# Two-layer graph network on one core: x1's third tile loaded among the attention weights, first residuals behind the weights, third tile's eviction moved

## The reference

```
h  = relu(layernorm(x))
n  = ln_weight * h * rsqrt(mean(h*h) + 1e-6)
g  = n @ W_root + bias + sum over r of (segment_sum of n[src] @ W_rel[r], by dst) / max(count_r, 1)
x1 = x + h + elu(g) @ wo

h  = relu(layernorm(x1))
p  = h @ W
e  = exp(-leaky_relu((p @ a_l)[src] + (p @ a_r)[dst], 0.1))
out = x1 + elu(segment_sum(e * p[dst], by src) / (segment_sum(e, by src) + 1e-5))
```

## Time and profile before

| | us |
|---|---|
| Median of 3 runs | 565.16 |
| The three runs | 562.09, 565.47, 565.16 |
| Profiled execution, whole time | 562.03 |
| Its span | 560.2 |
| PE busy | 529.5 (95%) |
| DVE busy | 401.2 (72%) |
| ACT busy | 226.4 (40%) |
| POOL busy | 74.4 (13%) |
| Granted TensorE clock, mean | 0.992 of full |

### The profile page before, as it was taken

How to read it: one execution, slowest core, us unless ns; L and a number is a source line. 1 busy time by engine, 2 the same in 40 slices (tenths; PEclk the granted TensorE clock), 3 DMA queues, 4 the chain that set the end, 5 groups by cost and what they waited for, 6 DMA issues and landing times.

```text
span 560.2 us, 8076 instructions
## 1 busy us (share of the span) xinstructions
PE 529.5 (95%) x3093; PEld 455.5 (81%) x3094; DVE 401.2 (72%) x662; ACT 226.4 (40%) x418; POOL 74.4 (13%) x69
## 2 busy tenths in 40 slices
PE   3989999999799999999997999999999999999996
PEld 2879898988688889989876888888877888888886
DVE  5846859549899898987486455556489887777643
ACT  5755335215745544445872233222233232222302
POOL 4063112000000000000000000000007222222310
PEclk9999999999899999999998999999999999999999
DMA  9842331303022124122594111110003322222221
GB/s 269 249 148 74 110 111 38 110 15 90 1 71 71 46 74 123 63 75 74 169 331 131 37 38 37 38 37 2 0 1 91 93 74 74 73 74 73 74 75 41
DMA packets 19805, 47.25 MB, mean 84 GB/s; under 512 B 3908, under 2 KB 8387, under 8 KB 19636
## 3 DMA queue, kind: packets, MB, share of 16 engines
q1 hardware_dynamic: 19761, 46.67, 27.5%
HBM read 31.30 MB, written 15.36 MB: 83 GB/s over the span
## 4 chain that ended last, share of the span: by engine, by line
PE 77%; DVE 12%; ACT 6%; DMA 2%; issue 2%; SPq 0%; DVEq 0%; ACTq 0%
PE ps L1178 10%; PE ps L1430 9%; PE ps L1432 8%; PE ps L1431 8%; PE ps L1339 8%; PE ps L1296 6%; PE ps L1412 5%; PE ps L1413 5%; PE ps L1411 5%; PE ps L1394 2%; PE ps L1382 2%; DVE bn L724 2%; PE ps L1384 2%; PE ps L1383 1%; DMA x1t<-x_scratch 1%
## 5 line engine op out<-in xcount | busy, mean ns | idle before, releaser
L1430 PE MATMUL ps<-h_hi,att_hi 125*125 125x512 f32 (+1 forms) x190 | 73.5, 387 | 0.0
L1431 PE MATMUL ps<-h_lo,att_hi 125*125 125x512 f32 (+1 forms) x190 | 72.6, 382 | 0.0
L1432 PE MATMUL ps<-h_hi,att_lo 125*125 125x512 f32 (+1 forms) x190 | 72.5, 382 | 0.0
L1411 PE MATMUL ps<-wg,gT_hi 128*125 128x512 f32 x160 | 64.3, 402 | 0.0
L1412 PE MATMUL ps<-wg,gT_hi 128*125 128x512 f32 x160 | 63.5, 397 | 0.0
L1413 PE MATMUL ps<-wg,gT_lo 128*125 128x512 f32 x160 | 63.4, 396 | 0.0
L1339 PE MATMUL ps<-msg_hi,adj_hi 125*125 125x288 f32 x200 | 55.8, 303 | 0.0
L543 ACT CAST adj_hi<-ps 125x400 fp32r<-125x400 f32 (+1 forms) x65 | 32.1, 494 | 52.4 <-PE ps L1296 51.3
L1339 PE MATMUL ps<-msg_lo,adj_hi 125*125 125x286 f32 x200 | 50.8, 294 | 0.0
L1178 PE MATMUL ps<-w_hi,hT_hi 128*125 128x430 f32 x128 | 46.3, 362 | 0.1
L1178 PE MATMUL ps<-w_hi,hT_lo 128*125 128x430 f32 x128 | 45.8, 358 | 0.0
(11 more groups left out here) (216 smaller groups left out, 1145.5 us busy)
## 6 DMA issues: line engine op xcount, KB each, us to landing
xt<-in_x SPq DMA_DIRECT2D x10, 448.0 KB
xh_scratch<-xt SPq DMA_DIRECT2D x10, 448.0 KB
xt<-xh_scratch SPq DMA_DIRECT2D x10, 448.0 KB
x_scratch<-xt SPq DMA_DIRECT2D x10, 448.0 KB
x1t<-x_scratch SPq DMA_DIRECT2D x10, 448.0 KB
xr<-x_scratch SPq DMA_DIRECT2D x10, 448.0 KB
out_x<-xr SPq DMA_DIRECT2D x19, 224.0 KB
wg_raw<-in_L_gnn_W SPq DMA_DIRECT2D x8, 512.0 KB, 6.2
```

The lines of the kernel that those rows point to most:

```text
L1411: M.matmul(to, hi, wg[k][:, 0, cut], start=n == 0, stop=False)
L1430: M.matmul(to, hi[:, s, :], h_hi[:, s, cut], start=s == 0, stop=False)
L1431: M.matmul(to, hi[:, s, :], h_lo[:, s, cut], start=False, stop=False)
L1432: return M.matmul(to, lo[:, s, :], h_hi[:, s, cut], start=False, stop=s == TILES - 1)
```

## The change

1. SP loads x1's tile 2 behind the first two attention weights, and tile 3 ahead of the store of x1's tile 9, instead of behind all of them.
2. POOL waits before its first residual until seven of the eight parts of `w_lo` are done.
3. In stage 1, tile 2's eviction (`transposed(2, 0, 1)`) and tile 0's messages stand ahead of the mean squares of tiles 2 and 3 on ACT; DVE's reciprocal of tile 2's mean square stands behind tile 0's messages.
4. At the seam, DVE does the statistics of tile 2 (`variance2`, then `deviation2`) and tile 1's `gT_lo` among the attention weights' lower parts, and ACT casts two weights before it evicts tile 1's transposes. The pipeline's `moments2` leaves tile 2 out.

The second branch of each engine's program (for inputs whose windows have more chunks than fixed) gets the same order; it isn't taken with these inputs.

```diff
--- before.py
+++ after.py
@@ -345,6 +345,7 @@
                     sp.wait_ge(S["rows_free"], 1)
                     for k in ORDER[0:2]:
                         load_wg(k)
+                    load_x1(2, 0)
                     sp.wait_ge(S["s_ps"], data(TILES - 1))
                     for k in ORDER[2:6]:
                         load_wg(k)
@@ -353,10 +354,12 @@
                         load_wg(k)
                     for first, end in ((0, BAND), (BAND, T)):
                         sp.dma_start(a_b[first:end], a_gat.rearrange("o (s d) -> (o s) d", s=2).partition_broadcast(end - first)).then_inc(S["a_in"], 16)
+                if t == TILES - 1:
+                    load_x1(3, 1)
                 store_x1(t, t % 2)
                 if t + 2 < TILES:
                     load_xh(t + 2, t % 2)
-            for t in range(2, TILES):
+            for t in range(4, TILES):
                 load_x1(t, t % 2)
 
             sp.wait_ge(S["h_dve"], data(TILES - 1))
@@ -418,6 +421,7 @@
                 sel = wsel[:].rearrange("v (w j) -> v w j", j=FIXED)
                 G.affine_select(out=sel, in_=sel, compare_op=ALU.not_equal, fill=1.0, base=0,
                                 pattern=[[-1, WINDOWS], [0, FIXED]], channel_multiplier=1).then_inc(S["more_consts"], 1)
+            pool.wait_ge(S["w_split"], KT - 1)
             for t in range(AHEAD):
                 residual(t, t % 2, t // 2)
             more_constants()
@@ -521,10 +525,10 @@
             norm(2, 0)
             deviation(3, 1)
             norm(3, 1)
+            transposed(2, 0, 1)
+            messages(0, 0, 0)
             mean_square(2, 0)
             mean_square(3, 1)
-            transposed(2, 0, 1)
-            messages(0, 0, 0)
             normed(4, 0, 2)
             messages(1, 1, 0)
             pads()
@@ -676,8 +680,8 @@
                 elu(*last)
                 counts_part(2)(*last)
                 y_split(*last)
+                split_gat_weights(range(0, 2))
                 transposed2(1, 1, 0)
-                split_gat_weights(range(0, 2))
                 second_layer()
             with act.If_ne(flag, 0):
                 split_wo()
@@ -885,10 +889,10 @@
             mean_square(1)
             deviation(2, 0)
             moments(3, 1, 1)
-            mean_square(2)
             low_parts(2, 0)
             dve.wait_ge(S["bias_in"], 16)
             messages(0, 0, 0)
+            mean_square(2)
             moments(4, 0, 2)
             messages(1, 1, 0)
             stage1(AHEAD, 5)
@@ -1104,8 +1108,12 @@
                     dve.wait_ge(S["el_rdy"], half(t, h))
                     V.scalar_tensor_tensor(xr[b][:, cut], em[b][:, cut], 1.0, xr[b][:, cut], ALU.min, ALU.add).then_inc(S["res_rdy"], 1)
             def second_layer():
-                split_gat_weights(range(2, KT))
-                pipeline((moments2, 0), (lambda t, b, d: transposed2(t, b, d) if t >= 2 else None, 1), (projected, 2),
+                split_gat_weights(range(2, 4))
+                transposed2(1, 1, 0)
+                split_gat_weights(range(4, 7))
+                deviation2(2, 0)
+                split_gat_weights(range(7, KT))
+                pipeline((lambda t, b, d: moments2(t, b, d) if t >= 3 else None, 0), (lambda t, b, d: transposed2(t, b, d) if t >= 2 else None, 1), (projected, 2),
                          closing=early_scores, after=TILES + 1, steps=(2, TILES + 2))
                 dve.wait_ge(S["logit_rdy"], data(TILES - 1))
                 first_scores(EARLY, TILES, "att_u", data(0), "att_v")
@@ -1139,8 +1147,8 @@
                 y_of(*last)
                 output1(*before)
                 y_split(*last)
-                transposed2(1, 1, 0)
                 split_gat_weights(range(0, 2))
+                variance2(2, 0)
                 output1(*last)
                 second_layer()
             with dve.If_ne(flags["dve"], 0):
```

## The result

| | before | after |
|---|---|---|
| Median, us | 563.53 (6 runs) | 556.80 (6 runs) |
| All runs, us | 562.08 to 565.47 | 556.24 to 557.65 |
| Ratio after / before | | 0.9879, 95% interval 0.9851 to 0.9906 |
| Profiled execution, span, us | 562.03, 560.2 | 556.86, 555.1 |
| Granted clock, mean | 0.992 | 0.995 |

The change gives 6.7 us, 1.2%, and the interval excludes no change. (The kernel before has six runs here, the three that are listed above and three more.) By the two profiled executions the last operation of DVE on the output starts at 550.61 instead of 556.64, 6.03 us earlier; the span is only 5.1 shorter because the last store took 0.9 us longer behind it. The 6.0 divide into 1.8 in layer 1 and 4.2 at the seam; between them, and from 310 us to the end, the two traces run in parallel.

What follows compares the result with a forecast made beforehand. TensorE's own work was taken to bound most of the span, with waits in a few places. A 1.0 plus B 4.1 gave 5.1 us, from the middle 563.7 to 558.6 us; range 555.6 to 562.5.

Steps and rivals of the forecast that it cites:

- A: Start of layer 1: POOL's wait and tile 2's earlier eviction together gain 1.0 us.
- by its own time: Counted from the profiled execution's 562.03 us, the forecast sum gives 556.9 us.
- A1: Start of layer 1: with POOL waiting, TensorE's wait for w_lo at 12 us goes; 0.44 us, floor 0, ceiling 1.3.
- rival 3: Start of layer 1: transposes also run at their later speed, 0.85 us more; total 5.9, 557.8 us; chance 0.09.
- A2: Layer 1, tile 2: eviction ahead of the squares starts when TensorE is done, 0.6 us sooner.
- A's other terms: Layer 1: later stores delay tile 4's load to near 30 us; costed at nothing, 1 us at worst.
- Rival 1: Layer 1: DVE cannot slip between two POOL residuals, so A = -1.3, total 2.8, 561.4 us; chance 0.12.
- B: Start of layer 2: tile 2's earlier x1 gains 4.1 us, 2.5 from TensorE's gap and 1.6 from the clock.
- Rival 2: Start of layer 2: weights come late behind tile 2's load; total 2.0 to 3.6, about 560.8 us; chance 0.10.
- a sign that I am wrong: Start of layer 2: ACT or DVE waiting for a weight's load would show the forecast wrong; no size given.
- Rival 4: Start of layer 2: late tile 2 load blocks DVE, TensorE one for one; 6.8 slower, 570.5; 0.05 shared with another rival.
- My two pairs: Whole kernel before: its four executions were taken to lie in two pairs, 3.1 us apart.

Runs made afterwards that it cites:

- Experiment 3: Two kernels, each the kernel before with one edit: POOL's wait alone, 561.86 us (ratio 0.995); tile 2's eviction moved alone, 563.31 us (0.9984).
- experiment 4: The changed kernel with POOL starting its residuals after four lower parts of the weights instead of seven: 560.49 us in one run.
- experiment 7: The kernel before with 14 unread matmuls ahead of tile 2's transposes at the seam: 563.71 us in one run.
- experiment 2: The kernel before with only the seam changed (loads and order on DVE, ACT and SP): 559.34 against 563.89 us, ratio 0.9901.
- experiment 6: The kernel before with only the two loads of x1 moved on SP: 560.2 us in one run.
- experiment 5: The changed kernel with x1's tile 2 loaded behind all weights, DVE's order kept: 571.08 us in one run.
- experiment 8: The kernel before with nine unread matmuls ahead of tile 3's transposes in layer 1: 562.61 against 563.57 us, ratio 0.9987.

## Why the prediction was right, and where it was not

The forecast's sum was 5.1 us and its number 558.6; the median is 556.8 and the gain 6.7. Sign, places and main mechanisms hold, and the size is short in A. At the seam the times are close: counted from tile 0's transposes, the third weight, the fifth weight and tile 2's transposes start within 0.1 us of the forecast. That the profiled execution took 556.86 where the sum gave 556.9 "by its own time" is luck: the kernel's work was 0.9 us further ahead, and the last store took it back. The chances gave 0.52 to a gain that can't be told from none and 0.45 to a clear one; it came out clear.

**A1, 0.44 forecast, 1.2 measured: the step that was mis-sized.** TensorE's wait at 12 went, as forecast. But the matmuls around it also run sooner at their later speed, by which tile 2's transposes start 1.20 us earlier. Counted from tile 0's transposes (8.90 before, 8.91 after), tile 1's start after 5.08 and 4.28: 0.80, of which 0.44 is the wait. Their own length fell by 0.40. I had this as rival 3 with 0.09, at 0.85 on top, and set it aside because "the same warm-up is in both programs"; it came with 0.76. That warm-up isn't a property of the program alone: with POOL's wait these transposes took 1.02 us in three traces and 1.46, 1.47, 1.61, 1.76 and 1.87 in five, the last where TensorE had waited 0.52 us ahead of its first products; in all six traces without it they took 1.87. So the 1.2 is one draw. From tile 0's transposes to tile 2's the seven traces with POOL's wait and TensorE's order unchanged need 22.22 to 23.78 us and the six without 24.05 to 24.25; against the 24.06 of the kernel before, A1 gives 0.3 to 1.8.

**A2, 0.60 forecast, 0.60 measured** (gap 1.95 to 1.35), but for half of the reason. I put the late eviction down to the squares' place. Experiment 3 shows that the squares were late because of the third hit on L763, and that POOL's wait alone moves it as much. My list of hits ended at 15 us; it should have gone on to the last residual that DVE meets. Since either edit closes the gap, the edits on ACT and DVE were not needed for these 0.60 once POOL waits.

**A's other terms.** The stores moved to 25.47 and tile 4's load to 28.61, and nothing waits for it: DVE's statistics start at 36.29, as costed at nothing.

**Rival 1** (A = -1.3, chance 0.12) did not come. L767 of tiles 2 and 3 takes 0.16 and 0.18 us amid the residuals. The rows show why it was closer than it looks: they start 0.09 us before the first residual's end (25.45) and 0.17 before the second's (27.80). Both engines start from the end of the last w_lo, one with residuals of 2.4 us and the other with a round of 2.27 us per tile, so they stay in step. With POOL's start moved by three weights (experiment 4) tile 3's L770 falls into a residual and is held 1.5 us. The last w_lo held the first residual for 0.8 us (3.20 instead of 2.4).

**B, 4.1 forecast, 4.2 to 4.3 measured.** The 2.5 of the gap and the 1.6 of the clock are both shown, the second alone by experiment 7. TensorE's gap for the fifth weight was 0.5 where I had 0.65. That so short a gap leaves the clock alone held, but the reason that I gave for it, that the 1.95 us in layer 1 had left it alone, doesn't: at the same place 1.94 us (experiment 2) and 1.76 us (experiments 6 and 7) did not. Two sentences of mine put too much on DVE: of the 4.29, 4.25 come with the two loads of SP (experiment 6), and the new order of statistics and low parts on DVE neither earns nor costs anything when the load is early. Rival 2 did not come: the weights land 0.8 us later in the median, and only the eighth makes ACT wait, 0.91 us. I had named such a wait as a sign that I am wrong; it isn't one here, since DVE takes this weight only 3.6 us after ACT is done with it (294.50 and 290.86).

**Rival 4** is a true mechanism and was priced too low. I counted one for one, and experiment 5 lost 13.3 us at the seam for a wait of 11.3: the low clock behind such a gap comes on top. The load took 12.9 us right behind the weights, not the 7.99 that I took as the worst of the trace.

**The rest of the gain**, 6.0 in the profiles against 6.7 in the medians. The profiled execution of before is among its fastest (562.03, where its six runs reach 565.47), and the traces show three places where executions of the same code differ. One is the gap in layer 1, behind which the clock falls or doesn't (1.3 to 1.6 us). One is the seam, where the late load makes a gap of 2.47 to 4.40 us in the five traces that have it, so that from tile 0's transposes to tile 3's 40.79 to 42.80 us pass; the four with the early loads and DVE's gT_lo not moved further need 37.34 to 37.38. The third is the stretch from 142 us on (experiment 8). The change acts on the first two; how they share the 0.7 is not shown. Against the first stands the eviction alone (experiment 3), which shortens the gap to the same 1.35 us and gained 0.9 us in all, 0.6 of it the gap itself. Five of the changed kernel's six runs are at 0.995 to 0.997. My two pairs, 3.1 us apart, were no pairs: more runs fill the space between them.

## What to carry to other kernels

Where an engine that shares a port runs long instructions beside short ones, list every short one that starts inside a long one, to the end of the stretch: one hit can be what makes another engine's order look wrong. Two edits that aim at one wait need not add; each alone may close it. Ask for a tile's data before a burst of loads and not behind it: here moving two requests past six loads gave two thirds of the gain, while reading it ahead of work that others wait for made the kernel 14 us slower than the changed one when the load came late.

## What the runs showed of the hardware

In layer 1, ahead of tile 3's transposes, a gap of TensorE of 1.95 us left the granted clock at 1.00 in the kernel before, and gaps of 1.94 us (experiment 2), 1.76 us (experiments 6 and 7) and 3.34 us (experiment 4) took it to 0.50, at a cost of 1.3 to 1.6 us. At the seam gaps of 2.47 to 4.40 us took it there in all five traces that have one, for 1.5 to 1.7 us. The gap of 1.35 or 1.36 us left it alone in all seven traces that have it, the one of 0.58 us in the one. The Trainium skill (TensorE: Matmul & The Clock Gate, Part 1) says that the point at which the clock changes is not tied to the program's start, so that the same kernel can show it differently from run to run; these traces agree.

The granted clock reads 1.00 from 8 to 16 us in every trace, though tile 1's transposes took from 1.02 to 1.87 us there: this column doesn't show the slow start.

GpSimd's additions and DVE's operations with two SBUF inputs, both ready, took turns one for one: 3.2 us for each of them in place of 2.4 and 1.04. An operation on one element per partition, 0.16 us alone, took 1.63 and 1.70 us: it was held to the end of the addition like a large one. VectorE's statistics, with one input, ran beside the residuals in their usual 1.26 to 1.28 us.
